# A gated graph network on one core: the states of 33 units transposed by VectorE blocks and DMAs through DRAM instead of by TensorE

## The chip, the cores and the metric

The kernel runs on one core of a Trainium2 chip. The metric is the device time of one launch in microseconds (us). The median of 3 runs of the kernel before is 760.96 us (760.62 to 761.38). The notes use TensorE, VectorE, ScalarE, GpSimd and SyncE for the engines that the profile calls PE, DVE, ACT, POOL and SP.

## What is computed

Sixteen graphs (B) of 512 nodes (N) with 128 features (D) pass through four layers, each followed by a residual sum and a layer norm. Layer 1 is five steps of a gated unit and takes most of the time:

```
def step(h, _):
    m_in = jnp.einsum('nm,bmd->bnd', in_matrix, h)
    m_out = jnp.einsum('nm,bmd->bnd', out_matrix, h)
    av = jnp.concatenate([m_in, m_out], axis=-1)
    u3 = h @ u3_w.T + u3_b
    z = jax.nn.sigmoid(av @ w3_w.T + w3_b + u3)
    r = jax.nn.sigmoid(av @ w4_w.T + w4_b + u3)
    hv = jnp.tanh(av @ w5_w.T + w5_b + (r * h @ u5_w.T + u5_b))
    h = (1.0 - z) * h + z * hv
...
x = _layernorm(x + L0(x, adj)); x = _layernorm(x + L1(x, adj, adj)); x = _layernorm(x + L2(x, adj)); x = _layernorm(x + L3(x, adj))
```

L0, L2 and L3 are one aggregation over the neighbours and one or two dense products each. `in_matrix` and `out_matrix` are the same matrix here.

## The kernel before, in words

A **unit** is one graph in one step: unit u is graph u % 16, and u // 16 says which layer or step. There are 128 units: 0 to 15 are L0, 16 to 95 the five gated steps, 96 to 111 L2, 112 to 127 L3. Every engine runs through the same list of **slots** s = 0, 1, 2, ... (`slot(s)`, one function for each engine), and in slot s it does the aggregation work of unit s and later parts of the units before. The order is thus written out by hand, and semaphores tie the engines together.

A graph is kept in two layouts. `feat[:, b, :]` has features on the partitions and the 512 nodes along the row. `nat_hi`/`nat_lo` have nodes on the partitions (four chunks of 128 nodes, T = 4) and are the stationary operands of the aggregation, a product with the adjacency matrix. Numbers are split in a high part (f32 rounded to fp32r) and a low part (the rest), and each product is three matmuls: high by high, high by low, low by high.

In slot s of the gated steps, TensorE does, in this order (lines 1028 to 1142):

- the aggregation of unit s, 12 matmuls of 128x512 (L1064 to L1066), stationary `nat_hi`/`nat_lo`, 
- the second half of the candidate of unit s-2, 3 matmuls on `reset_hi`/`reset_lo` (L1072, printed as L973 to L975),
- the gate of unit s-1: 3 matmuls on `feat_hi`/`feat_lo`, 3 on `agg_hi`/`agg_lo` (L1085, L1087); ScalarE reads this PSUM bank as the reset gate r,
- the first half of the candidate of unit s-1, 3 matmuls (L1089),
- the **turn**: four 128x128 transposes of the state of unit s-4 into `turn_ps` (L1103); in other slots other things are turned, and in two slots of the gated steps, 88 and 93, nothing is,
- 3 matmuls that turn the sum of r in the same bank into the sum of the update gate z (L1142). They wait until ScalarE has read r (`r_made`, L1141).

So one slot holds 27 matmuls of 128x512 and four transposes. ScalarE does in a slot: `gate_z` (s-2), `agg_hi` (s), the tanh `cand` (s-2), `gate_r` (s-1), `feat_hi` (s), `reset_hi` (s-1), and `nat_hi` of unit s-4 out of `turn_ps` (L518). VectorE does `agg_lo` (s), three operations on `cand` and `feat` that make the new state of s-2 (L822, L826, L829), `gate_r` times state (L834), `feat_lo`, `reset_lo`, and `nat_lo` of unit s-4 (L848). The new `nat_hi`/`nat_lo` of unit u are first used by the aggregation of unit u+16, that is in slot u+16. SyncE only issues DMAs; in the gated steps it has almost nothing to do. L0's slots also hold norms, splits of the rows into `nat_hi`/`nat_lo` (L463, L877; L540, L696 for the inputs) and bias seeds.

The state of unit u is made in slot u+2 (`state_made`); `STATE_LAG = 4` places its turn in slot u+4. The two `cand` buffers alternate by u % 2: the tanh of u (L486) waits for `state_made` of u-2.

Of the kernel before, what the change touches and what calls it, by code (L numbers as in the profile page):

```python
# [22 lines left out]
P = 128  # L23
# [17 lines left out]
LAST = B * STEPS  # L41
AFTER = B * (STEPS + 1)
# [88 lines left out]
def turns_at(s):  # L131
# [3 lines left out]
    if is_inner(s - STATE_LAG):  # L135
        found.append(("state", s - STATE_LAG))
# [37 lines left out]

def flat(v):
    return v.rearrange("p a n -> p (a n)")


def graph_layers(nc, x, adj, w0, b0, w3, b3, u3, ub3, w4, b4, w5, b5, u5, ub5, w2, b2, wl3, e, bl3, mix_dram, d_dram, out):
    with ExitStack() as ctx:  # L180
# [11 lines left out]
        nat_hi = sb("nat_hi", [P, B, T, D], F32R)  # L192
        nat_lo = sb("nat_lo", [P, B, T, D], F32R)
# [114 lines left out]
        turned = sem("turned")  # L308
        turn_read, turn_read_act, rows_read = sem("turn_read"), sem("turn_read_act"), sem("rows_read")
# [31 lines left out]
        def _(sp):  # L341
# [56 lines left out]

            sp.wait_ge(mix_loaded, 16)
# [19 lines left out]
        def _(act):  # L419
# [26 lines left out]
            def slot(s):  # L446
# [67 lines left out]
                if is_inner(u):  # L514
# [3 lines left out]
                    act.activation(nat_hi[:, u % B, :, :], turn_ps[k % 2][:, :].rearrange("p (t d) -> p t d", t=T),  # L518
# [142 lines left out]
        def _(dve):  # L661
# [50 lines left out]
            def slot(s):  # L712
# [133 lines left out]
                if is_inner(u):  # L846
                    dve.wait_ge(state_hi_made, u - B + 1)
                    dve.tensor_tensor(nat_lo[:, u % B, :, :],  # L848
                                      turn_ps[TURN_NO["state", u] % 2][:, :].rearrange("p (t d) -> p t d", t=T),
                                      nat_hi[:, u % B, :, :].bitcast(F32), ALU.subtract).then_inc(turn_read, 1)  # L850
# [94 lines left out]
        def _(pe):  # L945
# [82 lines left out]
            def slot(s):  # L1028

                if s < UNITS:  # L1030
# [3 lines left out]
                    elif 2 * B <= s < AFTER:  # L1034
                        pe.wait_ge(turn_read, reads(TURN_NO["state", s - B]))
# [12 lines left out]
                    if s == 0:  # L1048
# [3 lines left out]
                        for k in range(T):  # L1052
                            pe.matmul(ps, nat_hi[:, b, k, :], m_hi[:, k, :], start=(k == 0), stop=False)
                        pe.wait_ge(x_lo_made, 1)
                        for k in range(T):
                            pe.matmul(ps, nat_lo[:, b, k, :], m_hi[:, k, :], start=False, stop=False)
                        pe.wait_ge(eye_lo_made, T)
                        for k in range(T):
                            last = pe.matmul(ps, nat_hi[:, b, k, :], m_lo[:, k, :], start=False, stop=(k == T - 1))
                    else:  # L1060
                        for k in range(T):
                            if s == AFTER + B:
                                pe.wait_ge(turn_read, reads(TURN_NO["mix", k]))
# [106 lines left out]
```

## Time and profile before

| | us |
|---|---|
| median of 3 runs | 760.96 |
| the profiled execution's own time | 760.57 |
| its span | 758.7 |
| PE busy in the span | 747.5 (99%) |
| DVE busy | 638.1 (84%) |
| ACT busy | 503.1 (66%) |
| DMA queue of SP: share of 16 engines | 6.5% |
| TensorE transposes of states, L1103 (x320) | 47.8 busy, 272 ns each |

The profiled execution is one run of the kernel; 1.9 us of its time lie outside the span. Busy times of PE are of pipelined instructions whose ends are modelled: in a stream, 128x512 matmuls are shown with 0.39 us each and start every 0.227 us. So the starts of the rows, not their lengths, tell what PE's work costs. A slot of the gated steps can be measured from one first aggregation matmul (L1064) to the next.

### The profile page before, as it was taken

The page shows a single profiled execution, that of the slowest core. Times are in us where ns is not written, and L with a number is a line of the kernel's source. Part 1 is how long each engine was busy: PE and PEld are TensorE (multiplying, and loading weights), DVE is VectorE, ACT ScalarE, POOL GpSimd, SP SyncE. Part 2 cuts the span into 40 slices and gives each one's busy share as a digit, 9 for nine tenths or more (in the row PEclk, how much of TensorE's full clock was granted, in tenths as well). Part 3 has the DMA queues.
Part 4 walks back from the last instruction along what each step waited for, and adds up shares of the span by engine and source line. Part 5 has one row for each costly group of instructions (what it writes and reads, how often), then busy time and mean ns, then how long its engine had stood idle before and what let it go on. Part 6 is the DMA issues. An engine that isn't in the chain of part 4 may idle for free.

```text
span 758.7 us, 11706 instructions
## 1 busy us (share of the span) xinstructions
PE 747.5 (99%) x3768; PEld 626.9 (83%) x3768; DVE 638.1 (84%) x1473; ACT 503.1 (66%) x1047; POOL 159.4 (21%) x307
## 2 busy tenths in 40 slices
PE   8999999999999999999999999999999999999996
PEld 7888788888888888888888888888888888788886
DVE  5899998888888998877777788777999999787775
ACT  4899777666666676666666666666587858864433
POOL 1878420000000000000000000000122257654333
PEclk9999999999999999999999999999999999999999
DMA  6500000000031001000000000000000000101112
GB/s 213 221 1 2 1 1 1 1 1 1 0 119 15 0 2 56 1 0 1 1 1 0 1 2 0 1 1 1 0 1 1 1 0 2 26 4 42 57 43 84
DMA packets 11612, 17.21 MB, mean 23 GB/s; under 512 B 4512, under 2 KB 6048, under 8 KB 10912
## 3 DMA queue, kind: packets, MB, share of 16 engines
q1 hardware_dynamic: 11552, 16.47, 6.5%
q8 instruction: 31, 0.51, 0.3%
q14 instruction: 29, 0.24, 0.1%
HBM read 9.12 MB, written 5.25 MB: 19 GB/s over the span
## 4 chain that ended last, share of the span: by engine, by line
PE 80%; DVE 9%; ACT 6%; POOL 2%; issue 2%; DMA 1%; SPq 0%; POOLq 0%; ACTq 0%; DVEq 0%
PE agg_ps L1064 12%; PE agg_ps L1066 12%; PE agg_ps L1065 12%; PE gate_ps L973 6%; PE gate_ps L975 6%; PE gate_ps L974 6%; PE cand_ps L973 4%; PE cand_ps L975 4%; PE cand_ps L974 4%; PE turn_ps L1103 4%; PE gate_ps L980 3%; PE cand_ps L980 3%; DVE stats L863 1%; ACT res L441 1%; PE turn_ps L1107 1%
## 5 line engine op out<-in xcount | busy, mean ns | idle before, releaser
L1064 PE MATMUL agg_ps<-adj_hi,nat_hi 128*128 128x512 f32 x384 | 152.1, 396 | 0.0
L1066 PE MATMUL agg_ps<-adj_hi,nat_lo 128*128 128x512 f32 x384 | 150.2, 391 | 0.0
L1065 PE MATMUL agg_ps<-adj_lo,nat_hi 128*128 128x512 f32 x384 | 149.6, 390 | 0.0
L642 POOL TENSOR_SCALAR shift<-mean_var 128x4 f32<-128x4 f32 x62 | 24.5, 396 | 408.8 <-DVE mean_var L867 406.7
L817 DVE TENSOR_TENSOR agg_lo<-agg_ps,agg_hi 128x512 fp32r<-128x512 f32 x80 | 55.1, 689 | 57.5 <-ACT agg_hi L476 57.5
L512 ACT ACTIVATE reset_hi<-gate_r 128x512 fp32r<-128x512 f32 x80 | 50.6, 633 | 78.1 <-DVE gate_r L834 78.1
L493 ACT ACTIVATE gate_r<-gate_ps,bias 128x512 f32<-128x512 f32 x80 | 55.2, 690 | 48.4 <-PE gate_ps L975 48.4
L1066 PEld LDWEIGHTS agg_ps<-adj_hi,nat_lo 128*128 128x128 f32 x384 | 72.1, 188 | 16.2
L1065 PEld LDWEIGHTS agg_ps<-adj_lo,nat_hi 128*128 128x128 f32 x384 | 72.2, 188 | 15.6
L1064 PEld LDWEIGHTS agg_ps<-adj_hi,nat_hi 128*128 128x128 f32 x384 | 72.1, 188 | 15.1
L476 ACT ACTIVATE agg_hi<-agg_ps 128x512 fp32r<-128x512 f32 x80 | 48.7, 608 | 44.0 <-PE agg_ps L1066 43.7
L644 POOL TENSOR_TENSOR rstd<-mean_var,half 128x4 f32<-128x4 f32 x62 | 69.2, 1116 | 5.2
L973 PE MATMUL gate_ps<-agg_hi,w_hi 128*128 128x512 f32 x160 | 69.5, 434 | 0.6 <-ACT gate_r L493 0.4
L975 PE MATMUL gate_ps<-agg_lo,w_hi 128*128 128x512 f32 x160 | 62.8, 393 | 0.0
L974 PE MATMUL gate_ps<-agg_hi,w_lo 128*128 128x512 f32 x160 | 62.7, 392 | 0.0
L843 DVE TENSOR_TENSOR reset_lo<-gate_r,reset_hi 128x512 fp32r<-128x512 f32 x80 | 55.4, 693 | 8.4 <-ACT reset_hi L512 0.7
L822 DVE TENSOR_TENSOR cand<-cand,feat 128x512 f32<-128x512 f32 x80 | 55.2, 690 | 4.6
L486 ACT ACTIVATE cand<-cand_ps,bias 128x512 f32<-128x512 f32 x80 | 55.2, 691 | 5.6
L826 DVE TENSOR_TENSOR cand<-cand,gate_z 128x512 f32<-128x512 f32 x80 | 55.4, 692 | 2.7
L829 DVE TENSOR_TENSOR feat<-feat,cand 128x512 f32<-128x512 f32 x80 | 55.3, 692 | 2.7
L838 DVE TENSOR_TENSOR feat_lo<-feat,feat_hi 128x512 fp32r<-128x512 f32 x80 | 54.7, 684 | 0.0
L834 DVE TENSOR_TENSOR gate_r<-gate_r,feat 128x512 f32<-128x512 f32 x80 | 54.7, 683 | 0.0
(205 smaller groups left out, 1753.8 us busy)
## 6 DMA issues: line engine op xcount, KB each, us to landing
res<-in_x SPq DMA_DIRECT2D x16, 256.0 KB, 5.7
out<-res SPq DMA_DIRECT2D x16, 256.0 KB, 2.0
rows<-in_adj SPq DMA_DIRECT2D x4, 256.0 KB, 3.9
adj_hi<-eye_hi SPq DMA_DIRECT2D x1, 1024.0 KB, 9.9
adj_lo<-eye_lo SPq DMA_DIRECT2D x1, 1024.0 KB, 11.7
later<-in_adj SPq DMA_DIRECT2D x1, 1024.0 KB, 6.4
mix_rows<-mix SPq DMA_DIRECT2D x1, 1024.0 KB, 7.9
later<-mix_rows SPq DMA_DIRECT2D x1, 1024.0 KB, 4.7
```

What stands on the lines that cost most here:

```text
L486: act.activation(cand[:, u % 2, :], cand_ps[u % 2][:, :], ACT.Tanh, bias=bias[:, B_H:B_H + 1]).then_inc(cand_made, 1)
L493: act.activation(gate_r[:, u % 2, :], gate_ps[u % 2][:, :], ACT.Sigmoid, bias=bias[:, B_R:B_R + 1]).then_inc(r_made, 1)
L644: pool.tensor_tensor(rstd[:, i % RING, :], r, half[:, :], ALU.pow).then_inc(rstd_made, 1)
L826: dve.tensor_tensor(cand[:, u % 2, :], cand[:, u % 2, :], gate_z[:, u % 2, :], ALU.mult).then_inc(move_made, 1)
L829: dve.tensor_tensor(feat[:, u % B, :], feat[:, u % B, :], cand[:, u % 2, :], ALU.add).then_inc(state_made, 1)
L843: dve.tensor_tensor(reset_lo[:, :], gate_r[:, u % 2, :], reset_hi[:, :].bitcast(F32), ALU.subtract).then_inc(reset_lo_made, 1)
L973: pe.matmul(ps, w_hi[:, w, :], hi, start=start, stop=False, skip_group_check=True)
L974: pe.matmul(ps, w_lo[:, w, :], hi, start=False, stop=False, skip_group_check=True)
L975: return pe.matmul(ps, w_hi[:, w, :], lo, start=False, stop=stop, skip_group_check=True)
L1064: pe.matmul(ps, nat_hi[:, b, k, :], m_hi[:, k, :], start=(k == 0), stop=False)
L1065: pe.matmul(ps, nat_hi[:, b, k, :], m_lo[:, k, :], start=False, stop=False)
L1066: last = pe.matmul(ps, nat_lo[:, b, k, :], m_hi[:, k, :], start=False, stop=(k == T - 1))
```

## The change

- **33 units** (`BY_DMA`, 45 to 77) are no longer turned by TensorE. The four transposes, ScalarE's copy out of `turn_ps` and VectorE's subtraction from `turn_ps` are gone for them. In slots 49 to 81 TensorE has no turn.
- In their place, in slot u+2, right after the state is complete and the slot's other work is done, VectorE transposes `feat` (128x512) in 32x32 blocks into the free buffer `cand[:, u % 2, :]` (STREAM_TRANSPOSE, 128x4x128; node chunk and block order permuted on the way, inner step 4 elements when it writes). SyncE then issues four DMAs of 32x512 from `cand` to a DRAM scratch `state_blocks` (rows of 2 KB), and, after the blocks of the next unit have gone out, four DMAs of 32x4x128 back into `nat_lo` (runs of 512 B), which move the blocks to their partitions.
- In slot u+5 (`SWAP_LAG`) ScalarE copies `nat_lo` (now the whole state) into `nat_hi`, after waiting for the DMAs in (`swap_in`), and VectorE subtracts in place: `nat_lo` = `nat_lo` - `nat_hi`.
- The tanh of unit u waits for the DMAs out of unit u-2 (`swap_out`) in place of `state_made`.
- The **layout** of `nat_hi` and `nat_lo` changes for all 128 units: [B, T, D] becomes [B, D, T]. Every stationary operand of the aggregation is now read with a step of 4 elements (16 bytes), and every other write of `nat_hi`/`nat_lo` (inputs, splits, turned states) writes with that step, and VectorE reads `nat_hi` with it.

```diff
+BY_DMA = range(45, 78)
+BLOCK = 32
+BLOCKS = P // BLOCK
...
-    if is_inner(s - STATE_LAG):
+    if is_inner(s - STATE_LAG) and s - STATE_LAG not in BY_DMA:
         found.append(("state", s - STATE_LAG))
...
+SWAP_LAG = 5
...
+def by_chunk(v):
+    return v.rearrange("p d t -> p t d")
...
-        nat_hi = sb("nat_hi", [P, B, T, D], F32R)
-        nat_lo = sb("nat_lo", [P, B, T, D], F32R)
+        nat_hi = sb("nat_hi", [P, B, D, T], F32R)
+        nat_lo = sb("nat_lo", [P, B, D, T], F32R)
...
+            def swap_back(u):
+                sp.wait_ge(swap_out[u % 2], swaps(u))
+                if u - 2 in BY_DMA:
+                    sp.wait_ge(swap_in[u % 2], swaps(u - 2))
+                rows_of = swap_dram[u % B].rearrange("(a i) (q c) -> q i a c", a=BLOCKS, q=BLOCKS)
+                for q in range(BLOCKS):
+                    sp.dma_start(nat_lo[q * BLOCK:(q + 1) * BLOCK, u % B].rearrange("i (a d) k -> i a (d k)", a=BLOCKS).bitcast(F32),
+                                 rows_of[q]).then_inc(swap_in[u % 2], 16)
+            for u in BY_DMA:
+                sp.wait_ge(swapped, nth(BY_DMA, u))
+                for a in range(BLOCKS):
+                    cut = slice(a * BLOCK, (a + 1) * BLOCK)
+                    sp.dma_start(swap_dram[u % B, cut, :], cand[cut, u % 2, :]).then_inc(swap_out[u % 2], 16)
+                if u - 1 in BY_DMA:
+                    swap_back(u - 1)
...
-                    if u >= B + 2:
+                    if u - 2 in BY_DMA:
+                        act.wait_ge(swap_out[u % 2], swaps(u - 2))
+                    elif u >= B + 2:
                         act.wait_ge(state_made, u - B - 1)
                     act.activation(cand[:, u % 2, :], cand_ps[u % 2][:, :], ACT.Tanh,
...
-                    act.activation(nat_hi[:, u % B, :, :], turn_ps[k % 2][:, :].rearrange("p (t d) -> p t d", t=T),
+                    act.activation(by_chunk(nat_hi[:, u % B]), turn_ps[k % 2][:, :].rearrange("p (t d) -> p t d", t=T),
+                u = s - SWAP_LAG
+                if u in BY_DMA:
+                    act.wait_ge(swap_in[u % 2], swaps(u))
+                    act.activation(flat(nat_hi[:, u % B]), flat(nat_lo[:, u % B]).bitcast(F32),
                                    ACT.Copy).then_inc(state_hi_made, 1)
...
+                u = s - SWAP_LAG
+                if u in BY_DMA:
+                    dve.wait_ge(state_hi_made, nth(PARTED, u))
+                    dve.tensor_tensor(flat(nat_lo[:, u % B]), flat(nat_lo[:, u % B]).bitcast(F32),
+                                      flat(nat_hi[:, u % B]).bitcast(F32), ALU.subtract).then_inc(swap_lo_made, 1)
+                u = s - 2
+                if u in BY_DMA:
+                    dve.wait_ge(state_made, u - B + 1)
+                    dve.transpose(cand[:, u % 2, :].rearrange("p (q d k) -> p k q d", q=BLOCKS, k=T),
+                                  feat[:, u % B, :].rearrange("p (k q i) -> p k q i", q=BLOCKS, k=T)).then_inc(swapped, 1)
...
-                            pe.matmul(ps, nat_hi[:, b, k, :], m_hi[:, k, :], start=(k == 0), stop=False)
-                            pe.matmul(ps, nat_hi[:, b, k, :], m_lo[:, k, :], start=False, stop=False)
-                            last = pe.matmul(ps, nat_lo[:, b, k, :], m_hi[:, k, :], start=False, stop=(k == T - 1))
+                            pe.matmul(ps, nat_hi[:, b, :, k], m_hi[:, k, :], start=(k == 0), stop=False)
+                            pe.matmul(ps, nat_hi[:, b, :, k], m_lo[:, k, :], start=False, stop=False)
+                            last = pe.matmul(ps, nat_lo[:, b, :, k], m_hi[:, k, :], start=False, stop=(k == T - 1))
```

TensorE in a gated slot, from the reset gate's last matmul to the next aggregation; before:

```order
L975 MATMUL gate_ps<-agg_lo,w_hi 128x512
L973 MATMUL cand_ps<-agg_hi,w_hi 128x512
L974 MATMUL cand_ps<-agg_hi,w_lo 128x512
L975 MATMUL cand_ps<-agg_lo,w_hi 128x512
L1103 MATMUL turn_ps<-ident,feat 128x128 x4
L973 MATMUL gate_ps<-agg_hi,w_hi 128x512
L974 MATMUL gate_ps<-agg_hi,w_lo 128x512
```

and in a slot from 49 to 81 after the change:

```order
L1030 MATMUL gate_ps1<-agg_lo,w_hi 128x512
L1028 MATMUL cand_ps1<-agg_hi,w_hi 128x512 [waits cand_made]
L1029 MATMUL cand_ps1<-agg_hi,w_lo 128x512
L1030 MATMUL cand_ps1<-agg_lo,w_hi 128x512
L1028 MATMUL gate_ps1<-agg_hi,w_hi 128x512 [waits r_made]
```

The four transposes are gone, and the wait for `r_made` now stands behind three matmuls only.

VectorE at the end of a slot and the start of the next; before:

```order
L843 TENSOR_TENSOR reset_lo<-gate_r,reset_hi 128x512 [waits reset_hi_made]
L848 TENSOR_TENSOR nat_lo<-turn_ps0,nat_hi 128x512 [waits state_hi_made]
L817 TENSOR_TENSOR agg_lo<-agg_ps0,agg_hi 128x512 [waits agg_hi_made]
L822 TENSOR_TENSOR cand<-cand,feat 128x512 [waits cand_made]
```

and after the change:

```order
L888 TENSOR_TENSOR reset_lo<-gate_r,reset_hi 128x512 [waits reset_hi_made]
L899 TENSOR_TENSOR nat_lo<-nat_lo,nat_hi 128x512 [waits state_hi_made]
L904 STREAM_TRANSPOSE cand<-feat 128x4x128 [waits state_made]
L862 TENSOR_TENSOR agg_lo<-agg_ps0,agg_hi 128x512 [waits agg_hi_made]
L867 TENSOR_TENSOR cand<-cand,feat 128x512 [waits cand_made]
```

One instruction more stands between `nat_lo` and the next `agg_lo`, so VectorE has nine operations in a slot where it had eight.

## Rows read from the trace of the kernel before

**Rows 1.** The page: busy time of each engine (us, share of the span, instructions).

```profile
PE 747.5 (99%) x3768; PEld 626.9 (83%) x3768; DVE 638.1 (84%) x1473; ACT 503.1 (66%) x1047; POOL 159.4 (21%) x307
```

**Rows 2.** Waits of PE's weight loads over the whole span: us in total, times, longest.

```profile
PEld gate_ps L973 <- ACT gate_r L493: 1.9, 3, 0.9
...
PEld cand_ps L973 <- DVE reset_lo L843: 1.5, 4, 0.5
```

**Rows 3.** Timeline, PE, slot 56 with a turn: start us, us, instruction.

```profile
344.32 0.39 PE L975 MATMUL gate_ps<-agg_lo,w_hi 128*128 128x512 f32 x1
...
345.23 0.60 PE L1103 MATMUL turn_ps<-ident,feat 128*128 128x128 f32 x4
345.59 0.48 PE L973 MATMUL gate_ps<-agg_hi,w_hi 128*128 128x512 f32 x1
345.90 0.39 PE L974 MATMUL gate_ps<-agg_hi,w_lo 128*128 128x512 f32 x1
```

**Rows 4.** Timeline, ACT, the same slot; in brackets the idle time before.

```profile
342.71 0.60 ACT L476 ACTIVATE agg_hi<-agg_ps 128x512 fp32r<-128x512 f32 x1 [0.74 <-PE agg_ps L1066]
...
344.75 0.69 ACT L493 ACTIVATE gate_r<-gate_ps,bias 128x512 f32<-128x512 f32 x1 [0.67 <-PE gate_ps L975]
```

**Rows 5.** Timeline, PE, slot 88 without a turn.

```profile
551.06 0.40 PE L1064 MATMUL agg_ps<-adj_hi,nat_hi 128*128 128x512 f32 x1
...
555.63 0.39 PE L975 MATMUL gate_ps<-agg_lo,w_hi 128*128 128x512 f32 x1
...
556.31 0.39 PE L975 MATMUL cand_ps<-agg_lo,w_hi 128*128 128x512 f32 x1
556.80 0.50 PE L973 MATMUL gate_ps<-agg_hi,w_hi 128*128 128x512 f32 x1
557.13 0.40 PE L974 MATMUL gate_ps<-agg_hi,w_lo 128*128 128x512 f32 x1
...
557.60 0.40 PE L1064 MATMUL agg_ps<-adj_hi,nat_hi 128*128 128x512 f32 x1
```

**Rows 6.** Timeline, PEld, the same slot: the load that waits for r.

```profile
556.80 0.19 PEld L973 LDWEIGHTS gate_ps<-agg_hi,w_hi 128*128 128x128 f32 x1 [0.52 <-ACT gate_r L493]
```

**Rows 7.** Timeline, PE: first aggregation matmul of slots 46 and 80.

```profile
273.73 0.40 PE L1064 MATMUL agg_ps<-adj_hi,nat_hi 128*128 128x512 f32 x1
...
498.24 0.40 PE L1064 MATMUL agg_ps<-adj_hi,nat_hi 128*128 128x512 f32 x1
```

**Rows 8.** Timeline, DVE, from nat_lo to agg_lo, and the next agg_lo.

```profile
341.55 0.68 DVE L848 TENSOR_TENSOR nat_lo<-turn_ps,nat_hi 128x512 fp32r<-128x512 f32 x1
343.34 0.69 DVE L817 TENSOR_TENSOR agg_lo<-agg_ps,agg_hi 128x512 fp32r<-128x512 f32 x1 [1.10 <-ACT agg_hi L476]
...
349.93 0.69 DVE L817 TENSOR_TENSOR agg_lo<-agg_ps,agg_hi 128x512 fp32r<-128x512 f32 x1 [1.09 <-ACT agg_hi L476]
```

**Rows 9.** Stretches, all engines: slots 88 and 93; us, busy (instructions), clock, DMA.

```profile
551.06:557.60 6.54, 6.44 (x29) 4.99 (x27) 6.26 (x17) 5.63 (x12) 1.70 (x4) 1.00 0.01 3
583.99:590.67 6.68, 6.58 (x28) 4.91 (x27) 6.46 (x17) 5.45 (x12) 2.22 (x4) 1.00 0.02 4
```

**Rows 10.** Groups by line and form, DVE: busy us, mean ns, idle before.

```profile
L838 DVE TENSOR_TENSOR feat_lo<-feat,feat_hi 128x512 fp32r<-128x512 f32 x80 | 54.7, 684 | 0.0
...
L893 DVE TENSOR_TENSOR_SCAN later<-later,cap 128x2048 bf16<-128x2048 bf16 x1 | 4.4, 4417 | 0.0
```

**Rows 11.** Timeline, PE: four transposes whose stationary operand is read with a step of 16 bytes.

```profile
656.33 0.64 PE L958 MATMUL turn_ps<-ident,later 128*128 128x128 f32 x4
```

**Rows 12.** Timeline, ACT, in L0, in the middle of a stretch with no idle time.

```profile
57.44 0.88 ACT L540 ACTIVATE nat_hi<-res 128x512 fp32r<-128x512 f32 x1
57.96 0.87 ACT L463 ACTIVATE nat_hi<-res 128x512 fp32r<-128x512 f32 x1
```

**Rows 13.** DMA issues: KB each, median us to landing; and SP's queue.

```profile
out<-res SPq DMA_DIRECT2D x16, 256.0 KB, 2.0
...
13.46 5.58 SPq L349 DMA_DIRECT2D res<-in_x  x11
```

More of the change, by code:

```diff
@@ L157, with swaps @@
 TURN_NO = {x: i for i, x in enumerate(TURNS)}
+SWAP_LAG = 5
+PARTED = sorted((u for u in range(B, LAST)), key=lambda u: (u + (SWAP_LAG if u in BY_DMA else STATE_LAG), u in BY_DMA))
+def swaps(u):
+    return 16 * BLOCKS * sum(v <= u and v % 2 == u % 2 for v in BY_DMA)
 def read_by_act(turn):
@@ L308, in graph_layers @@
         turned = sem("turned")
+        swapped, swap_lo_made = sem("swapped"), sem("swap_lo_made")
+        swap_out, swap_in = ([sem(f"{n}{i}") for i in range(2)] for n in ("swap_out", "swap_in"))
         turn_read, turn_read_act, rows_read = sem("turn_read"), sem("turn_read_act"), sem("rows_read")
@@ L513, in slot @@
                 u = s - STATE_LAG
-                if is_inner(u):
+                if is_inner(u) and u not in BY_DMA:
                     k = TURN_NO["state", u]
@@ L695, in x_lo @@
                 dve.wait_ge(x_hi_made, b + 1)
-                dve.tensor_tensor(nat_lo[:, b, :, :], res[:, b, :, :], nat_hi[:, b, :, :].bitcast(F32),
+                dve.tensor_tensor(by_chunk(nat_lo[:, b]), res[:, b, :, :], by_chunk(nat_hi[:, b]).bitcast(F32),
                                   ALU.subtract).then_inc(x_lo_made, 1)
@@ L1034, in slot @@
                     elif 2 * B <= s < AFTER:
-                        pe.wait_ge(turn_read, reads(TURN_NO["state", s - B]))
+                        if s - B in BY_DMA:
+                            pe.wait_ge(swap_lo_made, nth(BY_DMA, s - B))
+                        else:
+                            pe.wait_ge(turn_read, reads(TURN_NO["state", s - B]))
                     else:
@@ L1052, in slot @@
                         for k in range(T):
-                            pe.matmul(ps, nat_hi[:, b, k, :], m_hi[:, k, :], start=(k == 0), stop=False)
+                            pe.matmul(ps, nat_hi[:, b, :, k], m_hi[:, k, :], start=(k == 0), stop=False)
                         pe.wait_ge(x_lo_made, 1)
                         for k in range(T):
-                            pe.matmul(ps, nat_lo[:, b, k, :], m_hi[:, k, :], start=False, stop=False)
+                            pe.matmul(ps, nat_lo[:, b, :, k], m_hi[:, k, :], start=False, stop=False)
                         pe.wait_ge(eye_lo_made, T)
                         for k in range(T):
-                            last = pe.matmul(ps, nat_hi[:, b, k, :], m_lo[:, k, :], start=False, stop=(k == T - 1))
+                            last = pe.matmul(ps, nat_hi[:, b, :, k], m_lo[:, k, :], start=False, stop=(k == T - 1))
                     else:
```

27 lines of the change are left out of this document (15 added, 12 removed).

## The prediction

> **What bounds the kernel now.** I read the page's busy times first, then the waits, then the order of time inside one slot. PE is busy 99% of the span [rows 1], and its weight loads wait for little: 1.9 us in 3 waits for the reset gate r (`gate_r`, L493), 1.5 us in 4 for `reset_lo` [rows 2]. That looks as if every matmul taken from PE came off the time. The timeline of one slot says otherwise. In slot 56 the last matmul of the reset gate starts at 344.32, ScalarE reads the gate from 344.75 for 0.69 us, that is until 345.44 [rows 3, 4], and only then may PE add the z part to the same bank. PE fills the time with three matmuls (0.68 us) and the four transposes, and its next z matmul starts at 345.59 [rows 3]. So the turn lies almost wholly in the shadow of ScalarE's read. Take it away and PE arrives at about 345.23, 0.2 us before r is read.
>
> The kernel has slots that show this: 88 and 93 have no turn. In slot 88 the z load comes with 0.52 us of idle time before it, put down to `gate_r` [rows 6]; the z matmul starts at 556.80, 1.17 us after the gate's last one at 555.63, where in slot 56 it was 1.27 [rows 3, 5]. The slot lasts 557.60 - 551.06 = 6.54 us [rows 5]. A slot with a turn lasts (498.24 - 273.73) / 34 = 6.603 us, mean of slots 46 to 79 [rows 7].
>
> **Removed: 33 turns.** By PE's own work a turn costs 6.603 less 27 x 0.227 (matmuls of 128x512 start 0.68 / 3 us apart, 555.63 to 556.31 [rows 5]), 0.47 us; 33 of them 15.6 us. By the trace most of that stays as a wait. Two readings of what is left: whole slots, 6.603 - 6.54 = 0.06 us; the chain from the gate's last matmul to the second z matmul, 1.58 us in slot 56 (344.32 to 345.90) and 1.50 in slot 88 (555.63 to 557.13), 0.08 us [rows 3, 5]. I take 0.07: 33 x 0.07 = **2.3 us less** (2.0 to 2.6).
>
> **Moved: ScalarE's `nat_hi`, VectorE's `nat_lo`.** They read SBUF in place of PSUM, same count, same place in the slot, one slot later. ScalarE has 0.74 us idle before `agg_hi` and 0.67 before `gate_r` [rows 4]; a copy that takes 0.1 us longer costs nothing. Slot 82 holds two such pairs (units 77 and 78), but no block transpose. If ScalarE's cover were gone, `agg_hi` and with it the r chain would slip by the excess.
>
> **Added: one block transpose (128x4x128) at the end of VectorE's slot.** No such instruction is in the trace. Behind it is queued the next `agg_lo`, then the state update. From `agg_lo` to `agg_lo` VectorE takes 6.59 us with 1.09 idle, so 5.50 of work [rows 8]; in a slot of 6.54 there is room for 1.04. Bounds from rows: 0.68 us, what a 128x512 operation takes on VectorE [rows 10]; and 1.10 us, 512 elements at the rate of the scan (4417 ns for 2048 elements, the slowest element rate there) [rows 10]. Two passes at the first row's time would be 1.37. I take 0.7, because it moves 512 elements once, like the first row: it fits, and costs **nothing**. With 1.10 the slot is 6.60 and VectorE the bound: (1.10 - 1.04) x 33 = 2 us, of which the first 0.8 are covered, since `reset_lo` comes early: in slot 56, which began at 273.73 + 10 x 6.603 = 339.76 [rows 7], PE uses it after 12 matmuls, near 342.5, and `nat_lo`, which stands behind it, starts at 341.55 [rows 8]; that takes back half of the gain. VectorE filled this far is no news: in slot 88 it is busy 6.26 of 6.54 us, and PE still met its 6.54 [rows 9]. In slot 93 it is busy 6.46 of 6.68, and that slot is 0.08 longer than one with a turn [rows 9]. The Trainium skill, Vector Engine (DVE) Microarchitecture Reference, section 3.8, has the block transpose sustain one element per cycle and lane, which agrees with the value taken; no run here shows it yet.
>
> **Added: eight DMAs and two waits.** SP's queue issues eleven DMAs in 5.58 us, 0.51 each, and 256 KB out lands 2.0 us after its issue [rows 13]. Eight issues are 4.1 us of a slot's 6.5: SP keeps up. I count from the moment VectorE has transposed unit u. `nat_lo` of VectorE's slot 55 starts at 341.55, 8.4 us after PE began slot 55 [rows 7, 8]; add 0.6 to the next operation and 0.7 for the transpose, and the moment lies 9.7 us after PE began slot u+2. The DMAs out are issued by +2.0 and landed by +4.0. The tanh of u+2 comes in slot u+4, behind `agg_hi`, that is at 343.3 - 339.8 = 3.5 us into the slot [rows 4, 7], or +6.9: slack 3 us. The DMAs in are issued behind the next unit's out, by +6.5 + 4.1, and landed by +12.6; `nat_hi` wants them in slot u+5, less than 1 us before `nat_lo`, near +17.5: slack 5 us. Both waits are then empty: **nothing**. If the cover fails, ScalarE stops at the tanh, and `gate_r`, PE's z part and all else stand behind it. PE uses the result eleven slots later still, in slot u+16.
>
> **Moved: the layout.** All aggregations, 128 x 12 = 1536 weight loads, now read with a step of 16 bytes. The trace has such loads: transposes whose stationary operand is stepped start every (0.64 - 0.28) / 3 = 0.12 us [rows 11], with a contiguous one every (0.60 - 0.27) / 3 = 0.11 [rows 3]. So 0.01 us more, where an aggregation matmul gives 0.227 us for the next load: hidden. It shows only where the first load of an aggregation follows narrow matmuls, in some 32 slots of L0 and L3: **0.3 us more**. The upper end is that each load delays its matmul by 0.01: 1536 x 0.012 = 18 us. The Trainium skill, SBUF — State Buffer, says that accesses which each fall on a new 16-byte line pay a penalty. It names no price; taken at the 18 us it would turn the forecast into 777. The trace agrees that a penalty exists (0.12 against 0.11) and not that it reaches the matmuls.
>
> ScalarE and VectorE now write the other `nat_hi`/`nat_lo` with that step. No row has such a write. The lower end is nothing. It would matter where they have no idle time: in L0 ScalarE starts 128x512 operations 0.52 us apart without a gap [rows 12], some 18 of them writes to `nat_hi`. Each 0.05 us more there is 0.9 us in all; twice the time, the upper end, 9.4 us. I take nothing, by the weight loads, which lost a tenth at most, and keep the rest for the range.
>
> **The sum** against the profiled execution's own 760.57: -2.3 + 0.3 = 758.6. The median of the runs is 0.4 above that execution, so **758.9 us** for the median, 0.3% faster. A measurement of this kernel can tell about 0.2% (1.5 us) from no change.
>
> **Rivals.**
> 1. *VectorE becomes the bound (slower).* The place is `agg_lo`, which waits behind the transpose; the point is 1.04 us, and from about 1.13 on (1.10 for the slot, the covered 0.8 us spread over 33) the kernel is slower than before. At two passes, 1.37 us: (1.37 - 1.04) x 33 - 0.8 = 10.1, giving 769. For it: slot 93, where a full VectorE made `reset_lo` late. Against: slot 88 with 6.26 busy [rows 9]. Chance 0.13.
> 2. *Stepped element-wise writes cost in L0.* For: ScalarE has no idle time there [rows 12]. Against: the small price of stepped loads. 0.05 us each gives 759.8, 0.26 each 763.6. Chance 0.2, half of it for less than 0.1 us each.
> 3. *Stepped weight loads reach the matmuls.* 18 us more, 777. Against: 0.1 us of cover for each. The SBUF page's rule would work this way. Chance 0.06.
> 4. *A DMA wait holds ScalarE.* The point is 3 us of delay in the DMAs out; from there each 0.1 us is 3.3 us in all, so 0.3 us past it gives 769. For: eight small DMAs a slot, rows of 2 KB and runs of 512 B where `out` moves whole 2 KB rows on 128 partitions. Chance 0.05.
> 5. *The whole turn is won.* PE does not wait for r, 33 x 0.47 = 15.6 us, 745. Against: slots 88 and 93. Chance 0.03.
>
> **The numbers.** The forecast has 0.53. Its own range is 757.9 to 759.9, so 0.07 of it falls within 0.2%; to that come 0.1 of rival 2 and 0.03 of rival 1 (a transpose near 1.1 us). Within 0.2%: 0.2. Faster: 0.46 of the forecast, 0.03 of rival 5, 0.01 of rival 2: 0.5. Slower: 0.3. The range goes from 757.2 to 766.0; it leaves out rival 5, rival 3, the dear ends of 1, 2 and 4, together 0.2.
>
> **What the new profile would show.** Right: slots 49 to 81 last 6.53 to 6.54 us; before nearly each z load (L1028) an idle time of about 0.5 us put down to `gate_r`, 33 times; the transpose near 0.7 us and VectorE still idle before `agg_lo`, 0.3 us; no wait of ScalarE on `swap_out` or `swap_in`; L0's slots unchanged. Wrong: a transpose over 1 us with PE waiting for `reset_lo`; aggregation matmuls that start more than 0.23 us apart; L0 slots above 4.10 us; ScalarE waiting for a DMA at `cand` or `nat_hi`; or 33 slots at 6.15.

## The result and the profile after

The changed kernel takes **792.05 us** (median of 4 runs, 791.92 to 793.27) where the kernel before takes 761.17 beside it: ratio **1.041** [1.039, 1.042]. It is slower by 31 us. The forecast was 758.9 with a range to 766.0, so the sign and the range were both wrong. The profiled execution took 791.98 us, span 790.0, at full clock in every stage.

The page after, busy times, beside [rows 1]:

```profile
PE 765.6 (97%) x3636; PEld 688.9 (87%) x3636; DVE 709.7 (90%) x1506; ACT 539.6 (68%) x1047; POOL 183.8 (23%) x307
```

PE has 132 instructions fewer (33 x 4 transposes), and its weight loads are busy 62 us longer. VectorE has 33 more and is busy 72 us longer, of which the block transposes are 36. ScalarE has the same 1047 and is busy 36.5 us longer. That is the sign of operations that have become slower, and the groups by line and form say which (columns as in [rows 10]: busy us, mean ns of one, idle before):

```profile
L1122 PEld LDWEIGHTS agg_ps<-adj_hi,nat_hi 128*128 128x128 f32 x384 | 118.8, 309 | 3.6
...
L501 ACT ACTIVATE nat_hi<-res 128x512 fp32r<-128x512 f32 x48 | 56.6, 1184 | 3.6 <-DVE res L856 3.6
...
L932 DVE TENSOR_TENSOR nat_lo<-res,nat_hi 128x512 fp32r<-128x512 f32 x48 | 51.6, 1078 | 0.0
...
L904 DVE STREAM_TRANSPOSE cand<-feat 128x512 f32<-128x512 f32 x33 | 36.2, 1098 | 0.0
L893 DVE TENSOR_TENSOR nat_lo<-turn_ps,nat_hi 128x512 fp32r<-128x512 f32 x31 | 34.0, 1097 | 9.2 <-ACT nat_hi L558 9.2
...
L558 ACT ACTIVATE nat_hi<-turn_ps 128x512 fp32r<-128x512 f32 x31 | 33.6, 1085 | 0.0
...
L899 DVE TENSOR_TENSOR nat_lo<-nat_lo,nat_hi 128x512 fp32r<-128x512 f32 x33 | 22.7, 687 | 0.0
L563 ACT ACTIVATE nat_hi<-nat_lo 128x512 fp32r<-128x512 f32 x33 | 20.4, 618 | 0.0
```

Every write with the 16-byte step takes 1.08 to 1.18 us, those of states and of rows alike, on both engines. The two of the 33 swapped units (L899, L563) write the same tensors without a step, and take 0.69 and 0.62. Groups of the kernel before for the writes of L501 and L558, with whole rows:

```profile
L463 ACT ACTIVATE nat_hi<-res 128x512 fp32r<-128x512 f32 x48 | 32.9, 689 | 2.8 <-DVE res L811 2.8
...
L518 ACT ACTIVATE nat_hi<-turn_ps 128x512 fp32r<-128x512 f32 x64 | 37.1, 580 | 0.0
```

Where that costs, two places show. In L0 ScalarE has no idle time; its timeline there, of after, beside [rows 12]:

```profile
70.12 1.39 ACT L585 ACTIVATE nat_hi<-res 128x512 fp32r<-128x512 f32 x1
71.03 1.40 ACT L501 ACTIVATE nat_hi<-res 128x512 fp32r<-128x512 f32 x1
71.96 0.90 ACT L506 ACTIVATE feat<-turn_ps 128x512 f32<-128x512 f32 x1
```

A write is 0.91 and 0.93 us from the next start where such operations stood 0.52 apart [rows 12]: 0.4 us more each, with no cover. The other place is one that the prediction did not look at, VectorE in the gated slots 40 to 47, where it also works on `later` and `eye_lo`. Slot 46 of after:

```profile
295.48 1.09 DVE L893 TENSOR_TENSOR nat_lo<-turn_ps,nat_hi 128x512 fp32r<-128x512 f32 x1 [0.28 <-ACT nat_hi L558]
296.48 0.75 DVE L969 SCALAR_TENSOR_TENSOR eye_lo<-later,row_d,eye_hi 128x512 fp32r<-128x512 f32 x1
```

and the same two before:

```profile
275.52 0.68 DVE L848 TENSOR_TENSOR nat_lo<-turn_ps,nat_hi 128x512 fp32r<-128x512 f32 x1
276.12 0.74 DVE L914 SCALAR_TENSOR_TENSOR eye_lo<-later,row_d,eye_hi 128x512 fp32r<-128x512 f32 x1
```

VectorE loses 0.40 us by its own stepped write and waits 0.28 for ScalarE's: 0.68 together. Slot 46 went from 6.61 to 7.34 us, since VectorE was busy 6.43 of the 6.61 there.

A slot of the swap, slot 53 of after (PE and its load; beside [rows 3, 5, 6]):

```profile
340.29 0.39 PE L1122 MATMUL agg_ps<-adj_hi,nat_hi 128*128 128x512 f32 x1
340.52 0.40 PE L1123 MATMUL agg_ps<-adj_lo,nat_hi 128*128 128x512 f32 x1
...
343.10 0.39 PE L1028 MATMUL cand_ps<-reset_hi,w_hi 128*128 128x512 f32 x1
...
344.94 0.39 PE L1030 MATMUL gate_ps<-agg_lo,w_hi 128*128 128x512 f32 x1
...
346.11 0.19 PEld L1028 LDWEIGHTS gate_ps<-agg_hi,w_hi 128*128 128x128 f32 x1 [0.52 <-ACT gate_r L533]
346.11 0.50 PE L1028 MATMUL gate_ps<-agg_hi,w_hi 128*128 128x512 f32 x1
...
346.92 0.39 PE L1122 MATMUL agg_ps<-adj_hi,nat_hi 128*128 128x512 f32 x1
```

The z load waits 0.52 us for the reset gate, as in slot 88, and z starts 1.17 us behind the gate's last matmul (344.94 to 346.11). But the twelve aggregation matmuls take 343.10 - 340.29 = 2.81 us, 0.234 each, against 0.227: the slot lasts 6.63 us, more than one with a turn before (6.60). VectorE and SP's queue in the same slot:

```profile
342.15 0.69 DVE L899 TENSOR_TENSOR nat_lo<-nat_lo,nat_hi 128x512 fp32r<-128x512 f32 x1
342.75 1.10 DVE L904 STREAM_TRANSPOSE cand<-feat 128x512 f32<-128x512 f32 x1
...
343.88 1.88 SPq L433 DMA_DIRECT2D state_blocks<-cand  x4
343.93 0.69 DVE L862 TENSOR_TENSOR agg_lo<-agg_ps,agg_hi 128x512 fp32r<-128x512 f32 x1
...
345.86 1.82 SPq L426 DMA_DIRECT2D nat_lo<-state_blocks  x4
```

SP issues the eight in 3.7 us, and the page gives 1.7 and 2.0 us to landing:

```profile
state_blocks<-cand SPq DMA_DIRECT2D x132, 64.0 KB, 1.7
nat_lo<-state_blocks SPq DMA_DIRECT2D x132, 64.0 KB, 2.0
```

None of ScalarE's waits is for these DMAs. What has grown is

```profile
PEld gate_ps L1028 <- ACT gate_r L533: 21.1, 40, 1.0
...
PEld cand_ps L1028 <- DVE reset_lo L888: 7.5, 18, 0.9
```

the two waits of [rows 2], 1.9 and 1.5 us before.

At the start of the swapped slots the new operation and the stepped write meet: in two slots VectorE has both the last stepped writes of turned states and the first block transposes. VectorE there:

```profile
311.42 0.66 DVE L862 TENSOR_TENSOR agg_lo<-agg_ps,agg_hi 128x512 fp32r<-128x512 f32 x1
...
316.40 1.10 DVE L893 TENSOR_TENSOR nat_lo<-turn_ps,nat_hi 128x512 fp32r<-128x512 f32 x1 [0.29 <-ACT nat_hi L558]
317.40 1.10 DVE L904 STREAM_TRANSPOSE cand<-feat 128x512 f32<-128x512 f32 x1
318.34 0.68 DVE L862 TENSOR_TENSOR agg_lo<-agg_ps,agg_hi 128x512 fp32r<-128x512 f32 x1
```

From one `agg_lo` to the next it takes 6.92 us, and its only idle time above 0.1 us is the 0.29 for ScalarE's stepped write. Slots 49 and 50 last 6.89 and 6.93 us, where they lasted 6.59 and 6.61 before.

### The profile page after: what moved, and what is told of

It is laid out like the page before. It is cut to its first block, busy times and chain, and to the rows that moved or that the text cites. A ratio compares the mean times of both kernels' runs of the same rounds, so it can differ in the third digit from the quotient of the medians.

```text
span 790.0 us, 11704 instructions
## 1 busy us (share of the span) xinstructions
PE 765.6 (97%) x3636; PEld 688.9 (87%) x3636; DVE 709.7 (90%) x1506; ACT 539.6 (68%) x1047; POOL 183.8 (23%) x307
## 4 chain that ended last, share of the span: by engine, by line
PE 50%; DVE 27%; ACT 16%; issue 5%; POOL 1%; DMA 1%; SPq 0%; POOLq 0%; ACTq 0%; DVEq 0%
PE agg_ps L1122 9%; PE agg_ps L1123 8%; PE agg_ps L1124 8%; PE gate_ps L1028 5%; PE gate_ps L1030 4%; PE gate_ps L1029 4%; DVE cand L871 3%; DVE feat L874 3%; ACT gate_r L533 3%; DVE cand L867 3%; ACT nat_hi L558 3%; DVE gate_r L879 3%; DVE agg_lo L862 2%; DVE nat_lo L893 2%; PE gate_ps L1035 2%
## 5 line engine op out<-in xcount | busy, mean ns | idle before, releaser
L1122 PE MATMUL agg_ps<-adj_hi,nat_hi 128*128 128x512 f32 x384 | 156.2, 407 | 0.0
L1123 PE MATMUL agg_ps<-adj_lo,nat_hi 128*128 128x512 f32 x384 | 152.6, 397 | 0.0
L1124 PE MATMUL agg_ps<-adj_hi,nat_lo 128*128 128x512 f32 x384 | 152.1, 396 | 0.0
L687 POOL TENSOR_SCALAR shift<-mean_var 128x4 f32<-128x4 f32 x62 | 37.9, 611 | 409.3 <-DVE mean_var L922 407.1
L1122 PEld LDWEIGHTS agg_ps<-adj_hi,nat_hi 128*128 128x128 f32 x384 | 118.8, 309 | 3.6
L1123 PEld LDWEIGHTS agg_ps<-adj_lo,nat_hi 128*128 128x128 f32 x384 | 119.2, 311 | 0.0
L1124 PEld LDWEIGHTS agg_ps<-adj_hi,nat_lo 128*128 128x128 f32 x384 | 118.9, 310 | 0.0
L501 ACT ACTIVATE nat_hi<-res 128x512 fp32r<-128x512 f32 x48 | 56.6, 1184 | 3.6 <-DVE res L856 3.6
L1122 PE MATMUL agg_ps<-eye_hi,nat_hi 128*128 128x512 f32 x124 | 55.0, 444 | 0.0
```

Source lines behind the costliest of these rows:

```text
L1122: pe.matmul(ps, nat_hi[:, b, :, k], m_hi[:, k, :], start=(k == 0), stop=False)
L1123: pe.matmul(ps, nat_hi[:, b, :, k], m_lo[:, k, :], start=False, stop=False)
L1124: last = pe.matmul(ps, nat_lo[:, b, :, k], m_hi[:, k, :], start=False, stop=(k == T - 1))
```

## The experiments

Theory A after the result: the layout costs all of it, and the swap itself works as forecast. Rivals: the step of the block transpose makes VectorE the bound; the DMAs delay something. Within A, reads (weight loads) and writes (element-wise) were to be told apart. Each kernel is compared with the kernel before on the same chip (760.6 to 760.9 us). The diffs of the layout and of the whole swap are against the changed kernel; those of the block transposes and of the filled slots are against the kernel told of just ahead of them. All are shortened.

**The layout alone.** No unit is swapped:

```diff
-BY_DMA = range(45, 78)
+BY_DMA = range(0)
...
-            swap_back(BY_DMA[-1])
```

> The new layout of nat_hi and nat_lo for all units, but no unit leaves TensorE: all 64 inner states are turned as before. Theory A (the layout costs the time): outside slots 49 to 81 the changed kernel's slots are about 29 us longer in sum than before, and those stay; slots 49 to 81 become like slots 82 to 91 of the changed kernel, 0.09 us each over before, 3 us. Together about 793 us. Rival B (the block transposes and DMAs cost it, by what they delay or by their traffic): under 770 us.

Measured: 793.38 us, ratio 1.044 [1.043, 1.046]. The layout costs 32.8 us, as expected, where the whole change costs 30.9: each is taken against its own kernel before, and the swap on top of the layout gains 1.9. In slots 49 to 81 of the two traces it gains 1.6; slots 49 and 50, above, are 0.2 us longer each than with the layout alone. (The profiled execution of this kernel took 3 us more than the median, all of it ahead of slot 1.)

**Only the reads stepped, only the writes stepped.** For reads only, the element-wise engines write whole rows, so the values that PE picks stand in another order; for writes only, PE loads whole rows of 128, likewise in another order. No unit is swapped in either. The amount of work is the same.

```diff
...
 def by_chunk(v):
-    return v.rearrange("p d t -> p t d")
+    return v.rearrange("p d t -> p (d t)").rearrange("p (t d) -> p t d", t=T)
```

> Layout of e1 for TensorE's weight loads alone: they read with a step of 16 bytes, ScalarE and VectorE write nat_hi and nat_lo as before in whole rows (the aggregation then uses values in the wrong order). A: loads of 310 ns as in the changed kernel; slots of L3 0.16 us longer, gated slots 0.09, so 15 us in sum, about 776 us. Rival (the loads are hidden, all comes from the writes): within 1 us of before.

```diff
-                            pe.matmul(ps, nat_hi[:, b, :, k], m_hi[:, k, :], start=(k == 0), stop=False)
+                            pe.matmul(ps, nat_hi[:, b].rearrange("p d t -> p (d t)")[:, k * D:(k + 1) * D], m_hi[:, k, :], start=(k == 0), stop=False)
...
```

> The other half: ScalarE and VectorE write (and VectorE reads) nat_hi and nat_lo with the step of 16 bytes, TensorE's weight loads read whole rows (values in the wrong order again). A: ScalarE's write 1.1 to 1.2 us in place of 0.6 to 0.7, VectorE's 1.1 in place of 0.7; L0 (slots 1 to 22) about 8 us longer, the slots that hold norms and L2's preparation another 6 to 8; about 776 us. With e6 it should add up to e1. Rival (the writes are hidden as VectorE and ScalarE have idle time): within 2 us of before.

Measured: reads alone 772.70 us, ratio 1.016 [1.014, 1.017], +12.1; writes alone 784.75, ratio 1.033 [1.031, 1.034], +24.2. I had expected about 776 for either: the reads cost 3 us less and the writes 9 more. Groups of reads only:

```profile
L1122 PEld LDWEIGHTS agg_ps<-adj_lo,nat_hi 128*128 128x128 f32 x384 | 119.4, 311 | 0.0
...
L557 ACT ACTIVATE nat_hi<-turn_ps 128x512 fp32r<-128x512 f32 x64 | 37.2, 581 | 0.0
```

and of writes only:

```profile
L1122 PEld LDWEIGHTS agg_ps<-adj_lo,nat_hi 128*128 128x128 f32 x384 | 72.2, 188 | 15.6
...
L557 ACT ACTIVATE nat_hi<-turn_ps 128x512 fp32r<-128x512 f32 x64 | 68.6, 1072 | 0.0
```

The loads go from 188 to 311 ns by the step of the reads, the writes from 0.58 to 1.07 us by the step of the writes, each alone. Both branches of the layout are real, and the writes are two thirds of it. (VectorE's operation both writes `nat_lo` and reads `nat_hi` with the step; the two were not told apart.) The sum of the two, 36.3, is more than both together, 32.8, and I had expected them to add up. The reading that fits, not tested by itself, is that a longer matmul costs nothing where PE already waits for a late write. By stages (from the first aggregation matmul of slots 1, 17, 49, 82, 109 and 127 in each trace; before in us, the others as differences to it; the last column is the last experiment):

| slots | before | after | layout alone | reads | writes | step of 8 bytes |
|---|---|---|---|---|---|---|
| 1-16 (L0) | 64.3 | +9.3 | +9.7 | +2.4 | +8.7 | +0.9 |
| 17-48 (gated) | 216.7 | +9.6 | +9.7 | +1.7 | +8.9 | +1.7 |
| 49-81 (gated, swap) | 217.9 | +1.3 | +3.0 | +3.0 | 0.0 | +1.9 |
| 82-108 (gated, L2) | 149.4 | +7.1 | +7.2 | +1.9 | +6.0 | +0.8 |
| 109-126 (L3) | 85.4 | +3.0 | +3.0 | +3.0 | 0.0 | +0.8 |

In slots 49 to 81 and in L3 the writes cost nothing: the engines have idle time there (0.7 us on ScalarE before `agg_hi` in a gated slot). Everywhere else they take most of the loss. In L0, all but 0.7 of their 8.7 us fall in slots in which ScalarE had no idle time before. Of the 14.9 us of slots 17 to 48 and 82 to 108, 8.6 fall in slots in which VectorE was busy for over 0.9 of the time before, and 2.1 in slots 102 and 104, in which ScalarE had no idle time (3.66 of 3.66 us and 3.70 of 3.70). Which wait took the rest was not looked at. The reads cost 0.09 us in each of the slots 49 to 81, that is 0.0075 us for each of twelve matmuls, and 0.16 in each of L3, 0.014 for each.

**The swap, one part at a time, in the old layout.** First only the turns go: no transposes on TensorE, 33 units keep stale `nat` values (their split still runs, on old contents), no block transpose, no DMAs.

```diff
-        nat_hi = sb("nat_hi", [P, B, D, T], F32R)
+        nat_hi = sb("nat_hi", [P, B, T, D], F32R)
...
-                    act.wait_ge(swap_in[u % 2], swaps(u))
+                    act.wait_ge(agg_done, u + 1)
...
```

> The kernel before with the 33 turns taken away and nothing in their place: no block transpose, no DMA, old layout; ScalarE and VectorE split what lies in nat_lo (so 33 states are not updated for the aggregation). It measures what the removal alone is worth. My forecast (the turn lies in the shadow of ScalarE's read of r): slots 49 to 81 of 6.53 us, 2.3 us less in all, 758.9 us, and an idle time of about 0.5 us before each z load. Rival (TensorE's own time counts): slots of 6.15, 746 us. Rival (nothing is won, another wait takes the place): 761.

Then a block transpose at its place in slot u+2, still with no DMAs, once with the output in runs of 32 elements and once with the step of 16 bytes:

```diff
+                    dve.transpose(cand[:, u % 2, :].rearrange("p (q k d) -> p k q d", q=BLOCKS, k=T),
+                                  feat[:, u % B, :].rearrange("p (k q i) -> p k q i", q=BLOCKS, k=T)).then_inc(swapped, 1)
```

> Run e3 (old layout, 33 turns gone, 758.0 us, slots of 6.51) plus the 33 block transposes of VectorE, written in whole runs of 32 elements, not with a step; no DMAs (their result is not used, the 33 states are not updated for the aggregation). Theory A (it is the step of 16 bytes in the write that makes the block transpose 1.10 us, as it made plain VectorE operations 1.09 in place of 0.68): transpose about 0.7 us, slots 49 to 81 stay at 6.51, 758 us. Rival B (a block transpose of 512 f32 elements takes 1.10 us by itself): VectorE has no idle time, slots of 6.63, about 762 us.

```diff
-                    dve.transpose(cand[:, u % 2, :].rearrange("p (q k d) -> p k q d", q=BLOCKS, k=T),
+                    dve.transpose(cand[:, u % 2, :].rearrange("p (q d k) -> p k q d", q=BLOCKS, k=T),
```

> Run e4 with one difference: the block transpose writes with the step of 16 bytes, as in the change. Both theories: 1.10 us, slots of 6.63 bound by VectorE, about 33 x 0.11 = 3.7 us over e3, 762 us. What tells is e4 against this one: A 4 us apart, B equal.

Last the whole swap with its DMAs. They land in a free buffer (`land`, the first half of `later`, whose own load moves behind the swaps), still in the order of blocks, and ScalarE's copy and VectorE's subtraction put runs of 32 in their places, so that no stepped access is left. All units are computed.

```diff
+        land = later[:, 0:2, :]
...
-                    sp.dma_start(nat_lo[q * BLOCK:(q + 1) * BLOCK, u % B].rearrange("i (a d) k -> i a (d k)", a=BLOCKS).bitcast(F32),
+                    sp.dma_start(land[q * BLOCK:(q + 1) * BLOCK, u % 2].rearrange("i (a c) -> i a c", a=BLOCKS),
...
-                    act.activation(flat(nat_hi[:, u % B]), flat(nat_lo[:, u % B]).bitcast(F32),
+                    act.activation(nat_hi[:, u % B].rearrange("p k (a d) -> p k a d", a=BLOCKS), land[:, u % 2].rearrange("p (a k d) -> p k a d", a=BLOCKS, k=T),
...
```

> The change in full, with all eight DMAs a unit, but without the step of 16 bytes anywhere: nat_hi and nat_lo keep the old layout, the block transpose writes runs of 32, the DMAs in land in a buffer of their own (runs of 512 bytes), and ScalarE and VectorE reorder runs of 32 elements when they read it. Everything is computed. A: DMAs and waits are hidden, so as e4: 758 us if the transpose is 0.7, 762 if it is 1.1. Rival C (the DMAs disturb: a wait of ScalarE on them, or the traffic slows the engines): slower than e4 by over 1.5 us.

| kernel | us | ratio | transpose, ns | slots 51-81, us |
|---|---|---|---|---|
| turns gone | 758.01 | 0.997 [0.996, 0.998] | none | 6.513 |
| + transpose, runs of 32 | 757.95 | 0.996 [0.995, 0.997] | 704 | 6.516 |
| + transpose, step of 16 bytes | 758.13 | 0.996 [0.995, 0.997] | 1081 | 6.517 |
| the whole swap, no steps | 757.82 | 0.996 [0.995, 0.997] | 704 | 6.515 |

All four are the same within the runs' spread. The block transpose is hidden at either length in the old layout, and so are DMAs and waits. So the swap in itself is worth 3 us, 33 slots x (6.603 - 6.515). That the stepped transpose would make VectorE the bound of these slots is refuted: I had expected 762. VectorE in the kernel with the stepped transpose:

```profile
341.10 0.69 DVE L891 TENSOR_TENSOR nat_lo<-nat_lo,nat_hi 128x512 fp32r<-128x512 f32 x1
341.70 1.09 DVE L896 STREAM_TRANSPOSE cand<-feat 128x512 f32<-128x512 f32 x1
342.78 0.69 DVE L854 TENSOR_TENSOR agg_lo<-agg_ps,agg_hi 128x512 fp32r<-128x512 f32 x1
```

`agg_lo` follows without a gap, and still the slot lasts 6.517. An operation shown as 0.69 lets the next one start 0.60 later, so the slack was larger than I read from lengths and idle times.

**Is the shadow worth something?** If the turn stood in the shadow of ScalarE's read of r, then its 0.47 us are to be had by putting other work there. Two of the next slot's aggregation matmuls are issued ahead of the z part in slots 49 to 81; first in the kernel with the turns gone:

```diff
+FILLED = range(49, 82)
+EARLY = 2
...
+                if s in FILLED:
+                    v = s + 1
...
+                    pe.matmul(ps, nat_hi[:, b, 0, :], adj_hi[:, 0, :], start=True, stop=False)
+                    if EARLY > 1:
+                        pe.matmul(ps, nat_hi[:, b, 0, :], adj_lo[:, 0, :], start=False, stop=False)
...
                     pe.wait_ge(r_made, u - B + 1)
```

> Run e3 (33 turns gone, nothing in their place) with two of the 12 matmuls of the next slot's aggregation issued ahead of the z part, in slots 49 to 81, so that TensorE works while ScalarE reads r. If the wait for r is what kept the turns' time (27 matmuls make 6.15 us, e3's slots are 6.51), the slots fall to 6.15 to 6.25 and the time to 746 to 749 us. Rival (VectorE or ScalarE sets the slot as soon as TensorE is faster): slots over 6.4, 755 us or more.

Then the same two matmuls are moved in the kernel with the whole swap and no steps:

> Run e2 (the whole swap with packed writes, 757.8 us) with e8's two matmuls of the next aggregation ahead of the z part in slots 49 to 81. Everything is computed. In e4 VectorE had 0.38 us idle in a slot of 6.51, so it needs 6.13 with the block transpose of 0.70, and TensorE needed 6.13 in e8: if both hold, slots of 6.14 to 6.2 and 746 to 748 us. Rival (two engines without idle time disturb each other, or the DMA traffic does): slots over 6.3, 751 us or more.

Measured: 745.48 us, ratio 0.980 [0.978, 0.981], and with the whole swap, everything computed, **745.50**, ratio 0.980 [0.978, 0.981]. PE in the latter:

```profile
341.60 0.39 PE L1035 MATMUL cand_ps<-agg_lo,w_hi 128*128 128x512 f32 x1
341.82 0.39 PE L1213 MATMUL agg_ps<-adj_hi,nat_hi 128*128 128x512 f32 x1
342.05 0.39 PE L1215 MATMUL agg_ps<-adj_lo,nat_hi 128*128 128x512 f32 x1
342.28 0.40 PE L1033 MATMUL gate_ps<-agg_hi,w_hi 128*128 128x512 f32 x1
...
347.95 0.39 PE L1213 MATMUL agg_ps<-adj_hi,nat_hi 128*128 128x512 f32 x1
```

The z part comes 0.23 us behind its neighbour, with no gap, and the slot lasts 347.95 - 341.82 = 6.13 us: 27 x 0.227. The wait of PE's loads for `gate_r` is back at 1.9 us over the whole span. What the change lacked was work to put into the time that it freed.

**The stepped transpose with the shadow filled**, the harder test of VectorE: slots of 6.13 leave it 0.4 us less. (33 states are stale here too.)

> Run e5 (block transpose with the step, 1.08 us, no DMAs, 33 states not updated for the aggregation) with the same two matmuls moved ahead. Theory (VectorE's own need, 6.13 with a transpose of 0.70, is 6.51 with one of 1.08): the move gives almost nothing, slots of 6.5 and about 758 us, with VectorE never idle. Rival (VectorE still has room): as e8, 745.5 us.

Measured: 746.73 us, ratio 0.981 [0.980, 0.983], not 758. VectorE from the transpose on:

```profile
345.77 1.09 DVE L898 STREAM_TRANSPOSE cand<-feat 128x512 f32<-128x512 f32 x1
346.73 0.66 DVE L856 TENSOR_TENSOR agg_lo<-agg_ps,agg_hi 128x512 fp32r<-128x512 f32 x1
```

It works without a gap, from one `agg_lo` (340.53) to the next (346.73) in 6.20 us here and in 6.17 on average, and now it does bound the slot: PE's slots last 6.165 us on average against 6.135 in the packed kernel. The step costs 1.2 us in the 33 slots (746.73 against 745.50). The operation behind `agg_lo` starts 0.60 us later here (340.53 to 341.13). In the kernel before it started 0.77 us later, from 343.34 [rows 8] to

```profile
344.11 0.69 DVE L822 TENSOR_TENSOR cand<-cand,feat 128x512 f32<-128x512 f32 x1
```

**More units.** The whole swap without steps and filled, again, with units 45 to 79 swapped and slots 49 to 83 filled; the diff is against that kernel with 33 units:

```diff
-BY_DMA = range(45, 78)
+BY_DMA = range(45, 80)
...
-FILLED = range(49, 82)
+FILLED = range(49, 84)
```

> Run e9 with two units more (45 to 79 in place of 45 to 77, matmuls ahead in slots 49 to 83). Two slots more at 6.14 in place of 6.60: 0.9 us less than e9. Rival (slots 82 and 83 are full already, the norms of the results begin): same as e9 or slower.

Measured: **744.83 us**, ratio 0.979 [0.977, 0.980], the fastest kernel here and 2.1% under the kernel before and 6.0% under the change's 792.05; 0.7 under the one with 33 units, where 0.9 was expected. The intervals of the ratios overlap, but the runs themselves do not (744.51 to 744.85 against 745.35 to 745.68, on one chip).

**How large a step hurts.** The layout alone again, with chunks interleaved in pairs, so that the step is 8 bytes:

```diff
-        nat_hi = sb("nat_hi", [P, B, D, T], F32R)
+        nat_hi = sb("nat_hi", [P, B, 2, D, 2], F32R)
...
```

> Run e1 (layout alone, all states turned by TensorE) with the chunks interleaved in pairs, so that nat_hi and nat_lo are read and written with a step of 8 bytes and not 16. Everything is computed. It asks at which step the price begins. If it begins as soon as neighbours are not adjacent: as e1, 793 us, writes of 1.1 us and loads of 310 ns. If it hangs on each access falling on a new 16 bytes: writes of 0.6 to 0.7, loads of 188 ns, 761 us. Or in between, half of it.

Measured: 766.88 us, ratio 1.008 [1.007, 1.009], +6.1, a fifth of what 16 bytes cost. Its groups:

```profile
L1098 PEld LDWEIGHTS agg_ps<-adj_hi,nat_hi 128*128 128x128 f32 x384 | 74.6, 194 | 14.9
...
L874 DVE TENSOR_TENSOR nat_lo<-turn_ps,nat_hi 128x512 fp32r<-128x512 f32 x64 | 43.8, 685 | 0.0
L544 ACT ACTIVATE nat_hi<-turn_ps 128x512 fp32r<-128x512 f32 x64 | 39.6, 618 | 0.0
```

With 8 bytes a write costs ScalarE 0.04 us more and VectorE nothing. The loads look almost as short as whole rows (194 ns), and still the aggregation matmuls of slots 49 to 81 start 0.233 us apart on average, against 0.229 in the kernel before and 0.235 with 16 bytes: the slots are 0.06 us longer, where 16 bytes made it 0.09. In L3 it is 0.05 against 0.16. So the length of a load in the trace does not say what it does to the matmuls.

## Why the prediction was wrong

- **The layout, writes: the step that failed most.** "I take nothing, by the weight loads, which lost a tenth at most" carried a price from TensorE's transposes over to ScalarE and VectorE. Measured, a stepped write costs 0.4 us more, +24.2 us in all. The upper end that I worked out, twice the time and 9.4 us, was right for L0 (+8.7), but I asked for a place without cover on ScalarE only. VectorE is nearly full in many of the slots 17 to 48 and 82 to 108 as well ([rows 9] shows 6.46 of 6.68 in slot 93), ScalarE in slots 102 and 104, and these two stretches brought 14.9 us that no case contained. Rival 2 was the mechanism, with at most 9.4 of the 24.2 us and a chance of 0.2.
- **The layout, reads.** Taken as 0.3 us by the row that shows 0.12 against 0.11 [rows 3, 11]; measured 12.1. The step that failed is "hidden": the loads were expected to stand behind 0.227 us of matmul. They are shown with 0.31 us, and the time grows by 0.0075 us a matmul in slots 49 to 81, by 0.014 in L3, by 0.008 over all 1536. The upper end named 0.01 a load but was multiplied with 0.012; with 0.01 it is 15.4 us and not 18. Rival 3 (0.06) was the mechanism. The Trainium skill, SBUF — State Buffer (Specifications), has lines of 16 bytes that want at least two hits each for full bandwidth, the penalty that I cited and set aside. The lengths in the traces agree, and on ScalarE and VectorE too: the step of 16 bytes, one hit a line, takes ScalarE's write from 0.58 to 1.07 us, the step of 8, two hits, to 0.62. The 6.1 us that the step of 8 bytes still costs do not follow from it. The Trainium skill, SBUF — State Buffer (Door 1: The DMA port swizzle), also says that one may step 4 fp32 for free; read as a step of 4 elements, that is what this change does, and the measurement decides against it.
- **Two costs that I gave 0.2 and 0.06 came together**, and they have one cause, the step of 16 bytes. They should have been one case with one chance.
- **The turn in ScalarE's shadow: right.** The z load waits 0.52 us, z comes 1.17 behind the gate, and a slot without steps lasts 6.51, 0.09 less than before, where I took 0.07: 3.0 us for 2.3. In the changed kernel the swap takes 0.07 from each of the slots 51 to 81, which last 6.627 where they last 6.693 with the layout alone. Rival 5 (the whole turn, 745) did not come about with the change, and its sum is what the filled kernel reaches: 745.5.
- **The block transpose.** 0.70 us with packed output, as taken; 1.10 as the change writes it. That this is also the upper bound is luck: the bound was the rate of a scan, and the length came from the step. Its cost, nothing, held at both in the old layout; in the changed kernel it cost 0.4 us, in slots 49 and 50, beside the stepped writes. The room of 1.04 and the turning point of 1.13 were too small. The 5.50 us left out the idle time before `agg_lo` alone, and held small waits further on: `cand` starts 0.77 us behind `agg_lo` in the kernel before and 0.60 in the filled kernel with the stepped transpose. There a whole slot's work with a transpose of 1.09 is 6.17 from start to start; 6.51 leaves 0.3. By these numbers, an estimate, rival 1 needed a transpose above about 1.4 us.
- **DMAs and waits: right.** 3.7 us of issue for 4.1 expected, no wait of ScalarE on them, and nothing lost in the whole swap without steps.
- **What would make it wrong** named aggregation matmuls more than 0.23 us apart and L0 slots above 4.10. Both came: 0.234, and, from slot 7 on, 4.26 to 6.7.

## What to carry to other kernels

Before a layout is changed for the sake of a few operations, list every operation in the program that reads or writes the tensor, and put a price on each form: here 33 units had a gain of 3 us, and all 128 units together paid 33 us for the new layout. A price for which the trace has no row on that engine stays open at its upper end, and the place where it counts is each stretch in which that engine is nearly full, not only the first one found. Work that stands in the shadow of a wait is worth its time only if independent work moves into its place: taking the turns out gave 3 us, and two matmuls put there 12 more.

## What the hardware showed

- ScalarE and VectorE writing 128x512 elements of 4 bytes: 0.58 to 0.72 us in whole rows, 1.07 to 1.21 with a step of 16 bytes, 0.62 to 0.75 with 8 (means of groups in the traces of before, the two layouts and writes only). The block transpose: 0.70 with output runs of 32 elements, 1.08 to 1.10 with the 16-byte step. VectorE's operation also reads `nat_hi` with the step; what the read alone costs was not tried.
- Weight loads of 128x128 are shown with 188 ns in whole rows, 194 at 8 bytes, 310 at 16. The aggregation matmuls behind them start 0.229, 0.233 and 0.235 us apart in slots 49 to 81 and 0.239, 0.242 and 0.253 in L3 (means of the kernel before and of the two layouts). Why a load of 194 ns delays them at all, and why the step of 16 bytes costs more in L3, stays open.
- Where nothing holds it, a VectorE operation starts some 0.09 us before the one ahead is shown to end (shown with 0.69 us, next start after 0.60). Its room in a slot is to be read from starts.
